# A graph kernel's first stage: the self weights go into the ring from ScalarE in place of POOL

## The chip, the cores and the metric

One core of a Trainium2 chip runs the kernel. The metric is the time of one execution on the device in microseconds (us). The runs of the kernel before took 4477.64, 4478.68 and 4486.39 us: a median of 4478.68.

## The reference

12500 nodes have 256 features each. 212500 edges (two directions of 100000 random pairs, and a self loop for each node) are sorted by their destination. What is computed, cut to what matters:

```python
# first stage (L0)
agg = segment_sum(x[src], dst, N)                     # 212500 rows of 256, float32
z = (1 + eps) * x + agg
z = relu(z @ W1 + b1) @ W2 + b2
z = (z - mean(z, 0)) * rsqrt(var(z, 0) + 1e-5) * gamma + beta + x
x1 = layernorm(x + z)
# second stage (L1)
s = segment_sum(edge_weight[:, None] * x1[src], dst, N)
out = layernorm(x1 + relu(s @ W3))
```

The second stage treats an edge from a node to itself apart: its weight goes on a diagonal. These sums of weights, one for each node, are the "self weights". They are gathered in the first stage, as a 257th column of its matmuls.

## The kernel before, in words

Edges are taken in pairs of chunks, 2 x 128 edges to a pair: 831 pairs, padded to 832. The nodes are 98 tiles of 128. A tile has some 8.5 pairs.

*The ring.* 32 slots of a pair each hold gathered rows of x. POOL fills them with indirect DMAs, two to a pair (gather, L552 to L555), in 26 rounds of 32 pairs. The first round stands ahead of the loop. In the loop (L574 to L587) POOL waits at each half ring for the indices (s_idx), and at each fourth slot for PE to have read the old rows (s_entered). Behind every eighth pair it runs selves_of (L565, L566): a copy of 128 x 16 numbers from self_next into the column ring_self of eight slots. The first four of these copies come from selfT, behind the first 64 gathers.

*SyncE.* follow (L450 to L468) waits for the four groups of eight pairs of a round (s_gathered), then for POOL's copy (s_selfed, L458), and then adds 8 to s_landed (L459), on which PE waits. Behind every second group it loads the next indices and the next self weights (self_next), 16 KB each.

*DVE.* It computes a table with ten numbers for each tile (NEW to SWEEP), which say where the tile's pairs begin and end; entry (L378) loads a tile's numbers into registers of an engine (L380). selfT, the self weights of all pairs, is computed before the first tile (L931 to L936). Then DVE works in blocks of two tiles (block, L1020): the first half of a sort (members), the one-hot matrices of the odd tile (ones_of_tile, L893 on; the operation stands in L901), the second half of the sort (places), and the one-hot matrices of the next even tile. Each set of one-hots has a short operation of 128 x 256 for the pair that two tiles share, one of 128 x 2048 for eight pairs, and a short one. Between the parts of a block stand operations for the sort's earlier block (keyed, L877 on) and the statistics of z (z_stats).

*PE.* sum_tile (L1270) multiplies the one-hots of a tile with the ring's rows and the 257th column (L1284, L1294), waits for s_onehot and s_landed, and puts other small matmuls in between; own adds the tile's own x.

*ACT.* two_tiles (L1675) copies sums out (summed), turns, applies ReLU and bias (hidden_out L1615, z_out L1625), hands the sort's ranks to DVE (ranks_out), and issues DMAs for x, z and the sort's runs. 49 blocks of two tiles make the stage.

After the stage come the normalisation, and the second stage with a like ring and gathers (L619), but without copies on POOL; its table has six numbers for an entry (entry2, L387).

Of the kernel before, what the change touches and what calls it, by code (L numbers as in the profile page):

```python
# [54 lines left out]
def gnn(nc, x, src, dst, edge_weight, w1, b1, w2, b2, gamma, beta, eps_gin, w3, lists, stage_dram, z_dram, x1_dram, out):  # L55
# [29 lines left out]
    with ctx:  # L85
# [48 lines left out]
        self_next = sb("self_next", [P, RING, 2], f32)  # L134
# [46 lines left out]
        row = work[0:1, 4000:4000 + 12 * (NT + 1)].rearrange("p (a t) -> p a t", a=12)  # L181
        row_i = work[0:1, 5200:5200 + 3 * NT].bitcast(i32).rearrange("p (a t) -> p a t", a=3)
        flag = sb("flag", [1, 3], f32)
        table = sb("table", [1, NT, 10], mybir.dt.uint16)
# [220 lines left out]
        NEW, HEAD, M4, M2, END, LOW, REP, SHARED, OFF, SWEEP = range(10)  # L405
# [6 lines left out]
        def _(sp):  # L412
# [37 lines left out]
            def follow(n_sweeps):  # L450

                with sp.Fori(0, n_sweeps) as sweep:
                    with sp.Fori(0, ROUNDS) as i:
                        r = sweep * ROUNDS + i
                        for g in range(4):
                            sp.wait_ge(s_gathered[g], r * (32 * QUARTER) + 32 * QUARTER)
                            stand(sp)
                            sp.wait_ge(s_selfed, r * 4 + g + 1)  # L458
                            sp.sem_inc(s_landed, QUARTER)  # L459
                            if g % 2 == 1:  # L460
                                h = g // 2
                                sp.dma_start(idx[:, h * HALF:(h + 1) * HALF, :],
                                             srcT[:, ds((i + 1) * RING + h * HALF, HALF), :]).then_inc(s_idx[h], 16)
                                sp.dma_start(self_next[:, h * HALF:(h + 1) * HALF, :],
                                             selfT[:, ds((i + 1) * RING + h * HALF, HALF), :]).then_inc(s_idx[h], 16)
                for h in range(2):
                    sp.wait_ge(s_idx[h], n_sweeps * (32 * ROUNDS) + 16)
                stand(sp)  # L468
# [70 lines left out]
        def _(pool):  # L539
# [25 lines left out]
            def selves_of(q, of):  # L565
                nc.gpsimd.tensor_copy(ring_self[:, q:q + QUARTER, :], of[:, q:q + QUARTER, :]).then_inc(s_selfed, 1)  # L566

            pool.wait_ge(s_selves, 1)
            for q in range(0, RING, QUARTER):
                selves_of(q, selfT)  # L570
# [3 lines left out]
            with pool.Fori(1, n_sweeps * ROUNDS) as r:  # L574
                for h in range(2):
                    pool.wait_ge(s_idx[h], r * 32 + 16)
                    stand(pool)
                    for q in range(h * HALF, (h + 1) * HALF):
                        if q % FOUR == 0:

                            pool.wait_ge(s_entered, r * RING + (q - RING + FOUR + 1))
                            stand(pool)
                        for c in range(2):
                            gather(q, c)
                        if (q + 1) % QUARTER == 0:
                            selves_of(q + 1 - QUARTER, self_next)
# [52 lines left out]
        def _(dve):  # L639
# [91 lines left out]
            sync()  # L731
            for column, of in ((NEW, newly), (HEAD, end), (M4, send), (M2, begins), (END, new), (LOW, slo)):
                setup(nc.vector.tensor_tensor(table[0:1, :, column], of, tmp, ALU.subtract))
# [159 lines left out]
            def ones_of_tile(j, bank):  # L893

                new, head, m4, m2, _, _, _, shared, off, sweep = entry(dve, j)
# [27 lines left out]
            def z_stats(m):  # L923
                dve.wait_ge(s_z, m + 1)
                stand(dve)
                for f in range(KH):
# [6 lines left out]
            setup(nc.vector.scalar_tensor_tensor(out=selfT[:, :, :], in0=selfT[:, :, :], scalar=0.0, in1=wT[:, :, :],  # L933
                                                 op0=ALU.is_equal, op1=ALU.mult))
            sync()
            nc.vector.tensor_copy(selfT[:, PADP:PADP + RING, :], selfT[:, 0:RING, :]).then_inc(s_selves, 1)  # L936
# [295 lines left out]
        def _(pe):  # L1232
# [37 lines left out]
            def sum_tile(j, bank, others):  # L1270

                new, head, m4, m2, end, low, rep, _, off, sweep = entry(pe, j)
# [23 lines left out]
                with pe.If(new < m4):  # L1296
                    with pe.Fori(new, m4, 2 * TWO) as p:
                        for b in range(0, 2 * TWO, TWO):
                            pe.wait_ge(s_landed, p + first + (b + TWO))
                            pe.wait_ge(s_onehot, p + counted + (b + TWO + 1))  # L1300
                            add(p + b, loop_of[:, b:b + TWO], TWO).then_inc(s_added, TWO)
                with pe.If(m4 < head):
                    pe.wait_ge(s_landed, m4 + first + TWO)
                    pe.wait_ge(s_onehot, m4 + counted + (TWO + 1))
                    add(m4, loop_of[:, 0:TWO], TWO).then_inc(s_added, TWO)
                pe.wait_ge(s_onehot, head + counted + TILE_ONES)
                pe.wait_ge(s_landed, low + first)
# [119 lines left out]
            pe.sem_inc(s_quarter, PARTS)  # L1427
            for k in range(5):
# [142 lines left out]
        def _(act):  # L1571
# [102 lines left out]

            def two_tiles(k, old, sorts=True, loads=True):  # L1675
# [6 lines left out]
                if loads:  # L1682
                    load_x(k + 1)
# [8 lines left out]
                if old >= 3:  # L1692
                    keep_z(k - 3)

            act.wait_ge(s_table, 1)
            act.wait_ge(s_selves, 1)
            for k in range(5):
# [184 lines left out]
```

## Time and profile before

| what | us |
|---|---|
| median of three runs | 4478.68 |
| the profiled execution, by the device's time | 4476.26 |
| its span in the trace | 4473.0 |
| POOL busy | 3318.0 (74%) |
| PE busy | 3437.8 (77%) |
| DVE busy | 2623.7 (59%) |
| ACT busy | 414.0 (9%) |

The span is that from the first to the last instruction of the trace, and the device's own time is 3.3 us longer. Times in rows are us from the span's start, unless they are marked ns or stand as a mean of one instruction, which is in ns. The first stage runs to about 2262 us, the second begins at 2429 us. An operation marked "DMA_INDIRECT" on POOL is the writing of descriptors for a gather, not the transfer. "issue" is time in which an engine waited for nothing that the profile shows. PEq, DVEq and so on are the sequencers of the engines.

### The profile page before, as it was taken

The numbers are of one execution on the slowest core, as the hardware profiler recorded it, in microseconds if no ns is written. First come the engines' busy times: TensorE is split into PE (matmuls) and PEld (weight loads), VectorE is DVE, ScalarE is ACT, GpSimd is POOL, SyncE is SP. The second block draws the span as 40 slices with busy tenths as digits, with TensorE's granted clock in tenths as the row PEclk, the third lists the DMA queues.
The fourth block names the chain that finished last, engine by engine and source line by source line (L and its number), as shares of the span: only waits on it lengthen the run. The fifth ranks groups of instructions, "written<-read, shape, count | busy, mean of one in ns | idle before, by whom it ended". The sixth has DMA issues, their size and how long they took to land.

```text
span 4473.0 us, 69589 instructions
## 1 busy us (share of the span) xinstructions
PE 3437.8 (77%) x16131; PEld 2829.6 (63%) x16132; DVE 2623.7 (59%) x5747; ACT 414.0 (9%) x1055; POOL 3318.0 (74%) x3456
## 2 busy tenths in 40 slices
PE   2787877877777777787654888888888888888887
PEld 2676766666666666666543666666666666666665
DVE  3888877776787777687656334344434444443443
ACT  0000000000000000000044000000000000000001
POOL 6777777777777777777734777777777777777775
PEclk7888988988988898888866999999999999999999
DMA  5343333433343333333386334434443444334343
GB/s 144 107 114 111 112 112 110 116 112 109 113 115 113 110 112 114 111 111 112 106 266 202 113 113 120 119 115 118 120 119 115 119 120 119 115 119 119 115 119 101
DMA packets 305380, 540.19 MB, mean 121 GB/s; under 512 B 85290, under 2 KB 197790, under 8 KB 305326
## 3 DMA queue, kind: packets, MB, share of 16 engines
q0 software_dynamic: 159424, 434.52, 33.5%
q10 hardware_dynamic: 89348, 67.77, 5.0%
q1 hardware_dynamic: 56554, 37.24, 2.8%
q8 instruction: 26, 0.43, 0.0%
q14 instruction: 28, 0.23, 0.0%
HBM read 489.80 MB, written 46.88 MB: 120 GB/s over the span
## 4 chain that ended last, share of the span: by engine, by line
POOL 62%; issue 22%; PE 5%; DVE 5%; DMA 3%; POOLq 1%; DVEq 1%; ACT 1%; ACTq 0%; SPq 0%; PEldq 0%
POOL ring L619 31%; POOL ring L553 30%; PE ps L1284 2%; PE ps L1494 1%; DMA x_dram<-ring 1%; DMA ring<-x_dram,idx 1%; DVE work L889 1%; POOLq L630 1%; PE ps L1367 1%; DVEq L380 1%; DMA z_dram<-z_pair 1%; DVE work L886 0%; ACT ring L1725 0%; DMA ring<-in_x,idx 0%; POOL ring L566 0%
## 5 line engine op out<-in xcount | busy, mean ns | idle before, releaser
L553 POOL DMA_INDIRECT ring<-in_x,idx x1664 | 1708.6, 1027 | 502.8 <-issue 473.1
L619 POOL DMA_INDIRECT ring<-x_dram,idx x1612 | 1524.0, 945 | 517.7 <-issue 489.8
L1494 PE MATMUL ps<-ring,work 128*128 x6448 | 1521.4, 391 | 339.8 <-SPq L529 337.8
L1494 PEld LDWEIGHTS ps<-ring,work 128*128 128x128 f32 x6448 | 1217.6, 193 | 629.4 <-issue 472.1
L1155 DVE TENSOR_SCALAR work<-ps,dstT,wT 128x256 f32<-128x256 f32 x1612 | 742.2, 539 | 1129.9 <-PE ps L1494 1057.9
L1284 PE MATMUL ps<-ring,ones_sb 128*128 x3324 | 935.8, 431 | 390.2 <-SPq L459 348.5
L1284 PEld LDWEIGHTS ps<-ring,ones_sb 128*128 128x128 f32 x3324 | 694.7, 216 | 549.2 <-issue 443.4
L901 DVE SCALAR_TENSOR_TENSOR ones_sb<-dstT,tile_base,minus_iota 128x256 f32<-128x256 f32 (+1 forms) x294 | 318.5, 1110 | 226.5 <-issue 187.3
L1367 PEld LDWEIGHTS ps<-work 128*128 128x128 f32 x3384 | 429.8, 197 | 17.9 <-DVE work L889 2.9
L1367 PE MATMUL ps<-work 128*128 128x128 f32 x3384 | 428.3, 279 | 2.1 <-DVE work L889 2.1
L886 DVE TENSOR_TENSOR work<-ps,current 128x768 f32<-128x768 f32 x282 | 267.8, 950 | 9.1 <-PE ps L1367 9.1
L889 DVE TENSOR_TENSOR work<-slot_is,ps 128x768 f32<-128x768 f32 x282 | 266.8, 946 | 0.0
L1294 PE MATMUL ps<-ring,ones_sb 128*128 x384 | 116.6, 429 | 61.6 <-issue 34.1
L1786 ACT ACTIVATE work<-ps 128x512 f32<-128x512 f32 x49 | 29.3, 597 | 1448.1 <-PE ps L1524 1448.1
L883 DVE TENSOR_TENSOR slot_is<-ps,current 128x384 f32<-128x384 f32 x282 | 156.0, 553 | 6.7
L1625 ACT ACTIVATE z_pair<-ps,cols 128x256 f32 (+1 forms) x98 | 41.1, 471 | 914.3 <-DVE zstats L927 848.3
L1294 PEld LDWEIGHTS ps<-ring,ones_sb 128*128 128x128 f32 x384 | 68.8, 199 | 86.7 <-issue 80.3
L811 DVE TENSOR_TENSOR ps<-ps,work 128x588 f32<-128x588 f32 x141 | 109.8, 778 | 20.7
L815 DVE TENSOR_REDUCE place_f<-ps 128x12 f32<-128x588 f32 x141 | 108.7, 771 | 20.6
L591 POOL DMA_INDIRECT lists<-work,target x47 | 45.4, 967 | 97.7 <-DMA lists<-work,target 73.1
L1451 PE MATMUL ps<-ident,ones_sb 128*128 128x128 f32 x196 | 47.0, 420 | 85.7 <-DVE ones_sb L1078 69.6
L1347 PE MATMUL ps<-hidT,w2s 128*128 128x256 f32 x392 | 106.3, 397 | 3.6 <-ACT hidT L1615 3.6
(245 smaller groups left out, 2178.6 us busy)
## 6 DMA issues: line engine op xcount, KB each, us to landing
ring<-in_x,idx POOLq DMA_INDIRECT x1664
ring<-x_dram,idx POOLq DMA_INDIRECT x1612, 2.7
z_dram<-z_pair ACTq DMA_DIRECT2D x49, 256.0 KB, 3.2
ones_sb<-x_dram ACTq DMA_DIRECT2D x49, 256.0 KB
ring<-z_dram SPq DMA_DIRECT2D x24, 512.0 KB, 6.0
ring<-in_x SPq DMA_DIRECT2D x24, 512.0 KB, 7.3
x_dram<-ring ACTq DMA_DIRECT2D x24, 512.0 KB, 3.8
out<-ones_sb ACTq DMA_DIRECT2D x48, 256.0 KB
```

Of the source, the lines that this page charges most:

```text
L553: nc.gpsimd.indirect_dma_start(out=ring[:, q, c, :], out_offset=None, in_=x, in_offset=bass.IndirectOffsetOnAxis(ap=idx[:, q, c:c + 1], ax ...
L619: nc.gpsimd.indirect_dma_start(out=ring[:, q, c, :], out_offset=None, in_=x1_dram, in_offset=bass.IndirectOffsetOnAxis(ap=idx[:, q, c:c + ...
L811: nc.vector.tensor_tensor(p_sel, p_base[:, q:q + 1, 0:NBK].to_broadcast([P, SPAN, NBK]), member[:, q * SPAN:(q + 1) * SPAN, :], ALU.mult). ...
L883: nc.vector.tensor_tensor(slot_is[:, q % 2, :, :], p_iota[:, 0:SLOTS].unsqueeze(1).to_broadcast([P, WIDTH, SLOTS]), current[:, 1, mine].un ...
L886: nc.vector.tensor_tensor(of_run[:, q, :, :], p_iota.unsqueeze(1).to_broadcast([P, WIDTH, P]), current[:, 0, mine].unsqueeze(2).to_broadca ...
L889: nc.vector.tensor_tensor(values[:, q, :, :, :], slot_is[:, q % 2, :, :].unsqueeze(3).to_broadcast([P, WIDTH, SLOTS, 2]), p_packed[:, :, m ...
L901: return nc.vector.scalar_tensor_tensor(out=to.rearrange("p b c n -> p (b c) n"), in0=dstT[:, ds(at, n), :].rearrange("p b c -> p (b c)"). ...
L1155: last = nc.vector.tensor_scalar(to[:, b, c, :], bucket_nodes, dstT[:, ds(at + b, 1), c], wT[:, ds(at + b, 1), c], ALU.is_equal, ALU.mult)
L1284: last = nc.tensor.matmul(wide, ones_of[:, b, c, :], summands[:, ds((p + b) & (RING - 1), 1), c, :].rearrange("p a d -> p (a d)"), start=F ...
L1294: nc.tensor.matmul(wide, shared_of[bank][:, 0, c, :], summands[:, ds((new + (RING - 1)) & (RING - 1), 1), c, :].rearrange("p a d -> p (a d)"),
L1367: last = nc.tensor.matmul(p_pack, of_run[:, q, c, :], values[:, q, c, :, :].rearrange("p n f -> p (n f)"), start=(q == 0 and c == 0), stop ...
L1494: last = nc.tensor.matmul(to[:, t * D:(t + 1) * D], ones_of[:, b, c, t * P:(t + 1) * P], ring[:, ds((p + b) & (RING - 1), 1), c, :].rearra ...
```

## The change

POOL makes no copies any more, and self_next, its 52 loads and SyncE's wait for the copies are gone. selfT is no longer continued beyond its end (the copy in L936 goes). The table has two more numbers for each tile, FROM and UPTO: the first and the last block of eight pairs that begins in the tile. ACT has a function selves, which loads the tile's entry, and for each such block waits until PE has read the slots' old rows, and copies 128 x 16 numbers from selfT into the ring. It is called for tiles 0 and 1 ahead of the loop, for tile 2k + 2 behind summed(k, 0), and for tile 2k + 3 at the end of two_tiles(k). PE waits for s_selfed itself. PE adds 32 to s_entered at its start, and the terms of POOL's wait change to match. All of PE's, DVE's and ACT's entry loads bring twelve numbers.

```diff
-        NEW, HEAD, M4, M2, END, LOW, REP, SHARED, OFF, SWEEP = range(10)
+        NEW, HEAD, M4, M2, END, LOW, REP, SHARED, OFF, SWEEP, FROM, UPTO = range(12)
...
                             sp.wait_ge(s_gathered[g], r * (32 * QUARTER) + 32 * QUARTER)
-                            stand(sp)
-                            sp.wait_ge(s_selfed, r * 4 + g + 1)
                             sp.sem_inc(s_landed, QUARTER)
...
-                                sp.dma_start(self_next[:, h * HALF:(h + 1) * HALF, :],
-                                             selfT[:, ds((i + 1) * RING + h * HALF, HALF), :]).then_inc(s_idx[h], 16)
...
-            def selves_of(q, of):
-                nc.gpsimd.tensor_copy(ring_self[:, q:q + QUARTER, :], of[:, q:q + QUARTER, :]).then_inc(s_selfed, 1)
-
-            pool.wait_ge(s_selves, 1)
-            for q in range(0, RING, QUARTER):
-                selves_of(q, selfT)
...
-                            pool.wait_ge(s_entered, r * RING + (q - RING + FOUR + 1))
+                            pool.wait_ge(s_entered, r * RING + (q + FOUR + 1))
                             stand(pool)
                         for c in range(2):
                             gather(q, c)
-                        if (q + 1) % QUARTER == 0:
-                            selves_of(q + 1 - QUARTER, self_next)
...
+            setup(nc.vector.scalar_tensor_tensor(out=from_i, in0=newly, scalar=float(QUARTER - 1), in1=tmp, op0=ALU.add, op1=ALU.subtract))
+            setup(nc.vector.scalar_tensor_tensor(out=upto_i, in0=new, scalar=float(QUARTER - 1), in1=tmp, op0=ALU.add, op1=ALU.subtract))
+            sync()
+            setup(nc.vector.tensor_scalar(from_i, from_i, 3, None, ALU.arith_shift_right))
+            setup(nc.vector.tensor_scalar(upto_i, upto_i, 3, None, ALU.arith_shift_right))
+            sync()
+            setup(nc.vector.tensor_copy(table[0:1, :, FROM], from_i))
+            setup(nc.vector.tensor_copy(table[0:1, :, UPTO], upto_i))
...
+                            stand(pe)
+                            pe.wait_ge(s_selfed, ((p + (b + TWO + QUARTER - 1)) >> 3) + sweep * 4)
                             add(p + b, loop_of[:, b:b + TWO], TWO).then_inc(s_added, TWO)
...
                 pe.wait_ge(s_onehot, head + counted + TILE_ONES)
+                stand(pe)
+                pe.wait_ge(s_selfed, upto + sweep * 4)
+                stand(pe)
                 pe.wait_ge(s_landed, low + first)
...
             pe.sem_inc(s_quarter, PARTS)
+            pe.sem_inc(s_entered, RING)
...
+            def selves(j):
+
+                *_, sweep, begin, upto = entry(act, j)
+                with act.If(begin < upto):
+                    with act.Fori(begin, upto) as b:
+                        act.wait_ge(s_entered, b * QUARTER + sweep * RING + (QUARTER + 1))
+                        stand(act)
+                        nc.scalar.activation(ring_self[:, ds((b & 3) * QUARTER, QUARTER), :], selfT[:, ds(nc.s_assert_within(b, 0, ROWS // QUARTER - 1, skip_runtime_bounds_check_because=IN_RANGE) * QUARTER, QUARTER), :], ACT.Copy).then_inc(s_selfed, 1)
+
             def two_tiles(k, old, sorts=True, loads=True):
...
                 summed(k, 0)
                 if loads:
+                    selves(2 * k + 2)
                     load_x(k + 1)
...
                     keep_z(k - 3)
+                if loads:
+                    selves(2 * k + 3)
 
             act.wait_ge(s_table, 1)
             act.wait_ge(s_selves, 1)
+            selves(0)
+            selves(1)
```

## Rows read from the trace of the kernel before

**Rows 1.** The page, part 4: the chain that ended last, shares by engine.

```profile
POOL 62%; issue 22%; PE 5%; DVE 5%; DMA 3%; POOLq 1%; DVEq 1%; ACT 1%; ACTq 0%; SPq 0%; PEldq 0%
```

**Rows 2.** Window of the first stage; columns: PE, PEld, DVE, ACT, POOL, PEclk, DMA.

```profile
90.00:2262.00 2172.00, 1674.13 (x8513) 1409.24 (x8514) 1634.04 (x3295) 166.22 (x524) 1669.13 (x1709) 0.87 0.39 112
```

**Rows 3.** Groups on POOL, 105 to 2235 us: busy, mean ns, idle before.

```profile
L553 POOL DMA_INDIRECT ring<-in_x,idx x1595 | 1636.7, 1026 | 470.7 <-issue 452.7 <-PE ps L1284 4.0
L566 POOL COPY ring<-self_next 128x16 f32<-128x16 f32 x99 | 23.2, 234 | 0.3
```

**Rows 4.** Waits, 105 to 2235 us: total us, times, longest us.

```profile
PE ps L1284 <- SPq L459: 301.3, 62, 14.3
...
POOL ring L553 <- PE ps L1284: 4.0, 13, 0.3
```

**Rows 5.** Second stage, the gathers: min/median/max ns, first and last start.

```profile
L619 POOL DMA_INDIRECT ring<-x_dram,idx x1612: 942/946/963, 2429.3 to 4443.1; - x180
```

**Rows 6.** Timeline of POOL, start us and us, around one copy.

```profile
1019.28 0.95 POOL L553 DMA_INDIRECT ring<-in_x,idx  x1 [0.30 <-issue]
1020.24 0.22 POOL L566 COPY ring<-self_next 128x16 f32<-128x16 f32 x1
...
1021.89 0.94 POOL L553 DMA_INDIRECT ring<-in_x,idx  x1 [0.31 <-issue]
```

**Rows 7.** Timeline of POOL, then of PE, at the start of the first stage.

```profile
93.30 0.61 POOL L566 COPY ring<-selfT 128x16 f32<-128x16 f32 x4
101.68 0.97 POOL L553 DMA_INDIRECT ring<-in_x,idx  x1 [7.77 <-PE ps L1284]
...
94.19 9.68 PE L1284 MATMUL ps<-ring,ones_sb 128*128 x36 [47.26 <-SPq L459]
```

**Rows 8.** Waits of SyncE's queue: us, times, longest.

```profile
SPq L459 <- POOL ring L566: 49.7, 1, 49.7
```

**Rows 9.** DVE by form, 105 to 2235 us: the long one-hot.

```profile
L901 DVE SCALAR_TENSOR_TENSOR ones_sb<-dstT,tile_base,minus_iota 128x2048 f32<-128x2048 f32 x96 | 227.2, 2366 | 4.3
```

**Rows 10.** Timeline of DVE: sets of one-hots, three early, two late.

```profile
408.77 3.32 DVE L901 SCALAR_TENSOR_TENSOR ones_sb<-dstT,tile_base,minus_iota 128x256 f32<-128x256 f32 x3 [2.81 <-issue]
...
426.59 3.29 DVE L901 SCALAR_TENSOR_TENSOR ones_sb<-dstT,tile_base,minus_iota 128x256 f32<-128x256 f32 x3 [1.02 <-issue]
...
451.42 3.33 DVE L901 SCALAR_TENSOR_TENSOR ones_sb<-dstT,tile_base,minus_iota 128x256 f32<-128x256 f32 x3 [2.82 <-issue]
...
2117.29 3.32 DVE L901 SCALAR_TENSOR_TENSOR ones_sb<-dstT,tile_base,minus_iota 128x256 f32<-128x256 f32 x3 [2.81 <-issue]
...
2135.10 3.29 DVE L901 SCALAR_TENSOR_TENSOR ones_sb<-dstT,tile_base,minus_iota 128x256 f32<-128x256 f32 x3 [1.01 <-issue]
```

**Rows 11.** Timeline of POOL beside the first two of these sets.

```profile
410.63 1.89 POOL L553 DMA_INDIRECT ring<-in_x,idx  x1 [0.30 <-issue]
...
426.70 1.19 POOL L553 DMA_INDIRECT ring<-in_x,idx  x1 [0.30 <-issue]
428.20 2.10 POOL L553 DMA_INDIRECT ring<-in_x,idx  x1 [0.30 <-issue]
```

**Rows 12.** One more set, DVE, and the gather beside it, POOL.

```profile
641.72 3.29 DVE L901 SCALAR_TENSOR_TENSOR ones_sb<-dstT,tile_base,minus_iota 128x256 f32<-128x256 f32 x3 [1.65 <-issue]
...
642.55 2.87 POOL L553 DMA_INDIRECT ring<-in_x,idx  x1 [0.30 <-issue]
```

**Rows 13.** Loads of a table entry, DVE: L380 ten values, L387 six.

```profile
L380 DVEq TENSOR_LOAD <-table x98: 2264/2270/3010, 48.2 to 2194.4; - x98
...
L387 DVEq TENSOR_LOAD <-table x49: 1383/1389/1398, 2425.5 to 4399.7; - x49
```

**Rows 14.** Timeline of ACT: two operations and the waits that end at them.

```profile
625.85 0.84 ACT L1615 ACTIVATE hidT<-ps,cols 128x256 f32<-128x256 f32 x2 [15.01 <-PE ps L1334]
...
652.59 0.84 ACT L1625 ACTIVATE z_pair<-ps,cols 128x256 f32 x2 [16.02 <-DVE zstats L927]
```

**Rows 15.** Chain in order of time near the end of the first stage.

```profile
2193.95 3.64 DMA ring<-in_x,idx
```

More of the change, by code:

```diff
@@ L133, in gnn @@
         minus_iota = sb("minus_iota", [P, P], f32)
-        self_next = sb("self_next", [P, RING, 2], f32)
         ranks_f = sb("ranks_f", [P, THIRDS + 1, NB1], f32)
@@ L180, in gnn @@
         unsorted_p = sb("unsorted_p", [P, 1], f32)
-        row = work[0:1, 4000:4000 + 12 * (NT + 1)].rearrange("p (a t) -> p a t", a=12)
-        row_i = work[0:1, 5200:5200 + 3 * NT].bitcast(i32).rearrange("p (a t) -> p a t", a=3)
+        row = work[0:1, 4000:4000 + 14 * (NT + 1)].rearrange("p (a t) -> p a t", a=14)
+        row_i = work[0:1, 5400:5400 + 5 * NT].bitcast(i32).rearrange("p (a t) -> p a t", a=5)
         flag = sb("flag", [1, 3], f32)
-        table = sb("table", [1, NT, 10], mybir.dt.uint16)
+        table = sb("table", [1, NT, 12], mybir.dt.uint16)
         sweeps = sb("sweeps", [1, 1], i32)
@@ L463, in follow @@
                                              srcT[:, ds((i + 1) * RING + h * HALF, HALF), :]).then_inc(s_idx[h], 16)
-                                sp.dma_start(self_next[:, h * HALF:(h + 1) * HALF, :],
-                                             selfT[:, ds((i + 1) * RING + h * HALF, HALF), :]).then_inc(s_idx[h], 16)
                 for h in range(2):
-                    sp.wait_ge(s_idx[h], n_sweeps * (32 * ROUNDS) + 16)
+                    sp.wait_ge(s_idx[h], n_sweeps * (16 * ROUNDS) + 16)
                 stand(sp)
@@ L575, in _ @@
                 for h in range(2):
-                    pool.wait_ge(s_idx[h], r * 32 + 16)
+                    pool.wait_ge(s_idx[h], r * 16 + 16)
                     stand(pool)
@@ L731, in _ @@
             sync()
+            from_i, upto_i = row_i[:, 3, :], row_i[:, 4, :]
+            setup(nc.vector.scalar_tensor_tensor(out=from_i, in0=newly, scalar=float(QUARTER - 1), in1=tmp, op0=ALU.add, op1=ALU.subtract))
[6 more added lines that the diff above has]
+            setup(nc.vector.tensor_copy(table[0:1, :, UPTO], upto_i))
             for column, of in ((NEW, newly), (HEAD, end), (M4, send), (M2, begins), (END, new), (LOW, slo)):
@@ L893, in ones_of_tile @@
             def ones_of_tile(j, bank):
-                new, head, m4, m2, _, _, _, shared, off, sweep = entry(dve, j)
+                new, head, m4, m2, _, _, _, shared, off, sweep, _, _ = entry(dve, j)
                 counted = sweep * RING + off
@@ L932, in _ @@
             sync()
[L933 to L936, printed above, removed]
+            nc.vector.scalar_tensor_tensor(out=selfT[:, :, :], in0=selfT[:, :, :], scalar=0.0, in1=wT[:, :, :],
+                                           op0=ALU.is_equal, op1=ALU.mult).then_inc(s_selves, 1)
             dve.wait_ge(s_selves, 1)
@@ L1270, in sum_tile @@
             def sum_tile(j, bank, others):
-                new, head, m4, m2, end, low, rep, _, off, sweep = entry(pe, j)
+                new, head, m4, m2, end, low, rep, _, off, sweep, _, upto = entry(pe, j)
                 first = sweep * RING
@@ L1304, in sum_tile @@
                     pe.wait_ge(s_onehot, m4 + counted + (TWO + 1))
+                    stand(pe)
+                    pe.wait_ge(s_selfed, ((m4 + (TWO + QUARTER - 1)) >> 3) + sweep * 4)
                     add(m4, loop_of[:, 0:TWO], TWO).then_inc(s_added, TWO)
                 pe.wait_ge(s_onehot, head + counted + TILE_ONES)
+                stand(pe)
+                pe.wait_ge(s_selfed, upto + sweep * 4)
+                stand(pe)
                 pe.wait_ge(s_landed, low + first)
```

## The prediction

> **What bounds the kernel now.** Read first the chain of waits: POOL holds 62% of it and "issue", the steps between POOL's instructions, most of the next 22% [rows 1]. Then the window of the first stage, 90 to 2262 us: POOL and PE are both about 77% busy, DVE 75%, ACT 8% [rows 2], so shares don't tell the bound. The waits do: PE waits 301 us for SyncE's report that rows have landed, POOL waits for PE 4.0 us in 13 places, each no longer than its usual gap [rows 4]. POOL sets the pace, by the number of gathers it can start.
>
> A gather's price is clearest in the second stage, where nothing else runs on POOL: (4443.1 - 2429.3) / 1611 = 1.25 us from start to start [rows 5]. In the first stage 1595 gathers take 2130 us, 1.335 us each. Two things explain the difference: the copies and the pauses. The pauses are 1636.7 us of busy time less 1595 x 0.946 [rows 3, 5] = 128 us; take off some 3 us for the slightly longer gather after each copy, and 125 us are left. They fall beside DVE's long one-hot operation, 96 times in the window, 2.37 us each [rows 9]: 1.30 us per tile. Each tile has one set of three L901 operations: a short one, the long one, a short one.
>
> **The parts of the change.**
>
> *Start of the stage.* POOL's four first copies stand at 93.30, behind its first 64 gathers; SyncE waits 49.7 us for them before it reports any landing [rows 8], PE begins at 94.19, and POOL then waits 7.77 us for PE to free slots [rows 7]. ACT can copy as soon as DVE's weights are ready, right before DVE's first entry load at 48.2 us [rows 13]; ACT's own load and the set of one-hots that PE needs too (load 2.3 to 2.7 us, set 3.3 us) end near 56, so PE begins there and is through tile 0 long before POOL needs the slots. POOL goes on at 93.6 in place of 101.68: -8.1 us. DVE's new operations on the 98-entry table (six, plus waits, some 1.5 us) and ACT's first two entries lie under POOL's first 64 gathers, and would cost PE's start no more than that if they did not.
>
> *100 copies inside the loop.* With a copy between, two gathers take 1021.89 - 1019.28 = 2.61 us instead of 2.50 [rows 6]: 0.11 us, not its 0.22 us of duration, as half of it fills the usual gap. 100 x 0.11 = -11 us. What POOL still waits for in these places (s_idx, s_entered) costs nothing: the second stage has the same kind of waits and a pitch of 1.25 throughout.
>
> *SyncE's queue.* 52 small loads and their waits go, and the wait for the copies; the landing reports come no later. Nothing else stands in that queue, and PE's waits are for gathers: 0.
>
> *ACT.* Two entry loads per block of two tiles, and 104 copies of 128 x 16. The nearest prices are DVE's load (2.27 us for ten values, [rows 13]) and POOL's copy (0.23 us, [rows 3]): some 3.5 us per tile. Behind them in ACT's queue are L1615 and L1625, which wait 15.0 and 16.0 us for PE and for DVE [rows 14]; these waits cover it. Without that cover see the third rival.
>
> *PE.* It gains waits on s_selfed, a longer entry load and register work, below 1 us per tile, under its 301 us of waits for landings. Only in the last tiles, where the chain runs through it from a landing at 2193.95 + 3.64 [rows 15], do I add 0.5 us. All of that tail follows the last gathers and so moves with POOL.
>
> *DVE and its effect on POOL.* This is the term that decides. Each tile's entry grows from ten values to twelve. The load takes 2.270 us for ten and 1.389 us for six [rows 13], 0.22 us a value, so 2.71 us for twelve: 0.44 us more before each set of one-hots. DVE alone can take it: its block of two tiles lasts (451.42 + 3.33) - (408.77 + 3.32) = 42.66 us when it waits for nothing, POOL's share of a block (831 pairs / 49 blocks x 2 x 1.335) is 45.3 us. But the pauses depend on where the long one-hot falls in POOL's 1.25 us cycle. POOL always resumes 0.73 us after a set's end: 412.09 and 412.82, 429.88 and 430.60, 645.01 and 645.72 [rows 10 to 12]. It then keeps its cycle until the next set. So the loss at a set is 0.72 us plus the remainder of (interval between set ends - 0.73 - 0.10 per copy) by 1.25; a remainder under about 0.2 counts with a whole 1.25 on top, for I find losses from 0.94 to 2.1. The rule gives 1.43 for the interval of 17.79 us and 1.01 for 24.87; the rows show 0.25 + 1.15 = 1.40 and 0.94, and 1.93 for a set that comes at another phase [rows 11, 12]. Of 95 intervals 32 are 17.8 us and 25 are 24.8 to 25.0, from the sets at 408.77 and 426.59 to those at 2117.29 and 2135.10 [rows 10].
>
> After the change they are 18.23 and 25.31 with no copy inside. (18.23 - 0.73) = 14 x 1.25 + 0.00: a loss of 1.97. (25.31 - 0.73) = 19 x 1.25 + 0.83: a loss of 1.55. So 32 x (1.97 - 1.40) + 25 x (1.55 - 0.94) = 33.5 us are lost again; I take 30, since DVE, no longer behind at the start, will have some six fewer regular intervals. The other 38 stay at their present mean. If the load cost nothing more, the missing copies alone would give 1.53 and 1.11: +8 us; with every phase equally likely the mean loss is 1.55 against 1.30: +24 us. All these are losses, because the present phases are among the best. Bounds of this term: 0 and +45.
>
> **Sum**, against the profiled execution's own 4476.3 us (span 4473.0): -8.1 - 11 + 30 + 0.5 = +11.4, that is 4487.7 us. The median of the runs shown, 4478.68, is 2.4 us higher; between the two I put the forecast at 4489 us.
>
> **Rivals.**
> 1. *The pauses keep their mean.* For it: the number of sets does not change. Against it: the arithmetic above, which fits the rows to 0.1 us. Time: 4476.3 - 19.1 + 2.4 = 4460 us, faster. The Trainium skill, "SBUF — State Buffer", section "Who interferes with whom", has a VectorE instruction with two SBUF inputs and a GpSimd instruction that reads SBUF exclude each other, the first to issue holding the ports for its whole length. The trace agrees that L901 stops gathers; a reader who only counts such instructions gets 98 before and after and would forecast this rival.
> 2. *The phases scatter*, because ACT's new loads coincide with DVE's and stretch them; DVE's take up to 3.01 us already [rows 13]. Then -19.1 + 24 + 0.5: 4482 to 4484 us, no difference that can be told.
> 3. *ACT becomes part of DVE's loop.* Place: the entry load of selves(2k + 3), between DVE's z statistics and ranks_f. It decides once ACT's 16.0 us of cover are gone. Price: DVE's block becomes 42.66 + 0.88 + 3.5 = 47.0 us against 45.3, times 47: about 4560 us. [rows 14] speak against it.
> 4. *PE does not begin earlier*, as something else holds tile 0. Then 8.1 us of gain are missing from any case.
>
> **How the numbers follow.** About 0.2% (9 us) is what a measurement of this kernel can tell from no change. The forecast has 0.48 and its own range 4480 to 4500 us; scattered phases 0.22; kept pauses 0.21; ACT in the loop 0.04; a late PE 0.05. Faster by over 0.2% (below 4469.7): nearly all of rival 1, 0.21. Slower by over 0.2% (above 4487.6): some two thirds of the forecast, a quarter of rival 2, rival 3, 0.43. Within: 0.36. The range that holds 8 in 10 takes in rival 1 at its lower end: 4459 to 4501 us.
>
> **What would show it.** In the profile after: PE's first L1284 near 56 us; POOL's first gather of the second round at about 93.6, no copy on POOL; 1.25 us between gathers outside the pauses; DVE's L380 load at 2.71 us; set intervals of 18.2 and 25.3 us; and a mean L553 gather above 1.026 us, near 1.04 to 1.05, where rival 1 has 1.02. The forecast is wrong if that mean does not rise, if the load's price does not grow with the values, or if PE's waits for landings disappear.

## The result and the profile after

The changed kernel takes 4496.85 us (median of 8 runs, 4493.98 to 4503.77), the kernel before in the same series 4483.6 us (8 runs, 4477.64 to 4488.28): a ratio of 1.0032, interval 1.0021 to 1.0043. It is 13.3 us slower. The profiled execution took 4497.28 us against 4476.26, a difference of 21.0 us, since the profiled execution of before was faster than all eight of its runs, 7.3 us below their median. What follows accounts for the difference of the two profiles; in the medians it is 13.3.

The page's chain and the window of the first stage, which answer to [rows 1, 2]:

```profile
POOL 64%; issue 22%; PE 7%; DMA 3%; POOLq 1%; ACT 1%; DVE 1%; ACTq 0%; SPq 0%; DVEq 0%; PEldq 0%
```

```profile
90.00:2262.00 2172.00, 1662.37 (x8330) 1398.38 (x8329) 1612.42 (x3256) 182.61 (x601) 1680.72 (x1606) 0.86 0.38 110
```

POOL is still what the chain hangs on. In the same 2172 us it is busy longer (1680.72 against 1669.13), though its copies are gone and it issued fewer gathers (1578 against 1595 from 105 to 2235 us). The group of gathers, 105 to 2235 us, as in [rows 3], then all gathers of the two stages (min/median/max ns, first and last start):

```profile
L548 POOL DMA_INDIRECT ring<-in_x,idx x1578 | 1652.6, 1047 | 480.6 <-issue 475.2 <-PE ps L1278 5.5
```

```profile
L548 POOL DMA_INDIRECT ring<-in_x,idx x1664: 942/946/3065, 7.0 to 2258.7; - x185
...
L606 POOL DMA_INDIRECT ring<-x_dram,idx x1612: 942/946/962, 2452.1 to 4465.9; - x180
```

A gather of the first stage now takes 1047 ns on average in place of 1026, at the same median of 946. The last one starts at 2258.7 us; before it was 2237.5. The second stage takes (4465.9 - 2452.1) = 2013.8 us, the same as in [rows 5] to 0.1 us. The waits of the stretch, which answer to [rows 4]:

```profile
POOL ring L548 <- issue: 475.2, 1560, 0.3
...
PE ps L1278 <- SPq L456: 271.6, 60, 14.5
...
PE ps L1278 <- DVE ones_sb L897: 10.0, 2, 7.9
...
PE ps L1278 <- ACT ring L1684: 10.8, 3, 5.7
```

PE still waits mostly for landings, and for ACT's copies (L1684) only 10.8 us in three places. The start of the stage, POOL, then DVE's third set of one-hots, then PE, then ACT; before, POOL ran its four copies at 93.30 and then waited until 101.68 [rows 7]:

```profile
84.30 2.91 POOL L548 DMA_INDIRECT ring<-in_x,idx  x1 [0.30 <-issue]
...
91.28 0.95 POOL L548 DMA_INDIRECT ring<-in_x,idx  x1 [0.30 <-issue]
92.53 0.95 POOL L548 DMA_INDIRECT ring<-in_x,idx  x1 [0.30 <-issue]
93.78 0.95 POOL L548 DMA_INDIRECT ring<-in_x,idx  x1 [0.30 <-issue]
95.03 0.95 POOL L548 DMA_INDIRECT ring<-in_x,idx  x1 [0.30 <-issue]
...
97.53 0.95 POOL L548 DMA_INDIRECT ring<-in_x,idx  x1 [0.30 <-issue]
```

```profile
83.50 3.29 DVE L897 SCALAR_TENSOR_TENSOR ones_sb<-dstT,tile_base,minus_iota 128x256 f32<-128x256 f32 x3 [3.09 <-issue]
```

```profile
58.19 2.08 PE L1278 MATMUL ps<-ring,ones_sb 128*128 x4 [8.15 <-ACT ring L1684]
```

```profile
53.70 0.23 ACT L1684 ACTIVATE ring<-selfT  x1 [23.79 <-issue]
54.45 0.23 ACT L1684 ACTIVATE ring<-selfT  x1 [0.53 <-issue]
57.83 0.23 ACT L1684 ACTIVATE ring<-selfT  x1 [3.14 <-issue]
```

The 7.77 us of waiting are gone. The gather at 97.53 is POOL's 65th, the first of the second round, which began at 101.68 before. It comes only 4.1 us earlier because DVE's third set, at 117.71 before, now falls among the first 64 gathers: the gather at 84.30 takes 2.91 us. The number of sets is 98 as before. The loads of a table entry on the three engines, to [rows 13], in ns:

```profile
L379 PEldq TENSOR_LOAD <-table x98: 2850/2856/3045, 46.6 to 2272.1; - x98
L379 ACTq TENSOR_LOAD <-table x98: 2535/2582/3457, 50.2 to 2267.9; - x98
L379 DVEq TENSOR_LOAD <-table x98: 2703/2710/3494, 50.5 to 2213.7; - x98
```

Three sets of one-hots on DVE in a row, and the gathers of POOL beside them:

```profile
1157.78 3.29 DVE L897 SCALAR_TENSOR_TENSOR ones_sb<-dstT,tile_base,minus_iota 128x256 f32<-128x256 f32 x3 [1.46 <-issue]
...
1183.14 3.27 DVE L897 SCALAR_TENSOR_TENSOR ones_sb<-dstT,tile_base,minus_iota 128x256 f32<-128x256 f32 x3 [3.25 <-issue]
...
1201.35 3.29 DVE L897 SCALAR_TENSOR_TENSOR ones_sb<-dstT,tile_base,minus_iota 128x256 f32<-128x256 f32 x3 [1.46 <-issue]
```

```profile
1158.61 2.89 POOL L548 DMA_INDIRECT ring<-in_x,idx  x1 [0.30 <-PE ps L1278]
1161.81 0.95 POOL L548 DMA_INDIRECT ring<-in_x,idx  x1 [0.30 <-issue]
...
1184.41 2.43 POOL L548 DMA_INDIRECT ring<-in_x,idx  x1 [0.30 <-issue]
1187.14 0.94 POOL L548 DMA_INDIRECT ring<-in_x,idx  x1 [0.30 <-issue]
...
1202.16 2.90 POOL L548 DMA_INDIRECT ring<-in_x,idx  x1 [0.30 <-issue]
1205.36 0.95 POOL L548 DMA_INDIRECT ring<-in_x,idx  x1 [0.30 <-issue]
```

The sets end at 1161.07, 1186.41 and 1204.64: intervals of 25.3 and 18.2 us. POOL goes on 0.74, 0.73 and 0.72 us after each end. The gather caught takes 2.89, 2.43 and 2.90 us instead of 0.95, losses of 1.94, 1.48 and 1.95 us. In [rows 11] the same two kinds of set cost 0.94 and 1.40.

**Where the 22.5 us of span went.** For every two neighbouring gathers of a trace I took the time from start to start less 1.25 us, and put it to a set of one-hots where one lies beside them:

| us | before | after | difference |
|---|---|---|---|
| beside the 98 sets | 125.9 | 163.7 | +37.8 |
| copies on POOL, and its wait at the start | 18.1 | 0 | -18.1 |
| other, start of the first gather | | | +1.5 |
| last gather to the end of the first stage | 24.4 | 27.5 | +3.1 |
| between the stages | 167.4 | 165.9 | -1.5 |

The sum is +22.8, against 22.5 in the spans (the rest is rounding). Of the 18.1 us the start is 8.1 and the 100 copies 10.0. The mean loss of a set rose from 1.28 to 1.67 us (96 and 95 sets). The difference by the device's time is 21.0 us and not 22.5, because that time is 3.3 us longer than the span before and 1.8 us after.

One thing is needed to read the experiments. They were measured in six series, each with the kernel before beside it, and each kernel is compared only with the kernel before of its own series. In five of the six the clock granted to TensorE was lower, 0.82 of full speed on average in place of 0.90, and the kernel before took 5376 to 5398 us in place of 4482. One of these five and the one at 0.90 report the same chip number, so it need not belong to a chip. The two levels are called "the low clock" and "the full clock" below; where an expectation speaks of two kinds of chip, it is these two. They are names and not a cause: among the eight runs of the changed kernel in the first series one had a mean granted clock of 0.797 and took 4503.77 us, only 7 us above the median. The changed kernel itself was never measured at the low clock.

### The profile page after: what moved, and what is told of

Same layout as the page of the kernel before. It is cut to its first block, busy times and chain, and to the rows that moved or that the text cites. A ratio compares the mean times of both kernels' runs of the same rounds, so it can differ in the third digit from the quotient of the medians.

```text
span 4495.5 us, 70641 instructions
## 1 busy us (share of the span) xinstructions
PE 3471.4 (77%) x16131; PEld 2855.9 (64%) x16132; DVE 2613.0 (58%) x5752; ACT 438.8 (10%) x1160; POOL 3331.5 (74%) x3352
## 4 chain that ended last, share of the span: by engine, by line
POOL 64%; issue 22%; PE 7%; DMA 3%; POOLq 1%; ACT 1%; DVE 1%; ACTq 0%; SPq 0%; DVEq 0%; PEldq 0%
POOL ring L548 32%; POOL ring L606 32%; PE ps L1278 4%; DMA ring<-in_x,idx 1%; PE ps L1368 1%; DMA x_dram<-ring 1%; PE ps L1496 1%; POOLq L617 1%; DMA z_dram<-z_pair 0%; DMA ring<-x_dram,idx 0%; ACT ring L1741 0%; PE ps L1348 0%; PE ps L1335 0%; POOLq L618 0%; PE ps L1288 0%
## 5 line engine op out<-in xcount | busy, mean ns | idle before, releaser
L548 POOL DMA_INDIRECT ring<-in_x,idx x1664 | 1746.0, 1049 | 510.5 <-issue 501.0
L1278 PE MATMUL ps<-ring,ones_sb 128*128 x3324 | 958.2, 439 | 359.1 <-SPq L456 280.8
L1278 PEld LDWEIGHTS ps<-ring,ones_sb 128*128 128x128 f32 x3324 | 711.1, 222 | 523.3 <-issue 412.4
L1368 PEld LDWEIGHTS ps<-work 128*128 128x128 f32 x3384 | 429.6, 197 | 14.8
L1368 PE MATMUL ps<-work 128*128 128x128 f32 x3384 | 427.6, 279 | 0.0
L1288 PE MATMUL ps<-ring,ones_sb 128*128 x384 | 117.0, 431 | 38.0 <-issue 36.4
L1273 PE MATMUL ps<-zeros 1*128 1x257 bf16 x98 | 26.3, 268 | 147.4 <-issue 113.6
L1348 PE MATMUL ps<-hidT,w2s 128*128 128x256 f32 x392 | 117.3, 430 | 3.0 <-ACT hidT L1617 3.0
```

Of the source, the lines that this page charges most:

```text
L548: nc.gpsimd.indirect_dma_start(out=ring[:, q, c, :], out_offset=None, in_=x, in_offset=bass.IndirectOffsetOnAxis(ap=idx[:, q, c:c + 1], ax ...
L1278: last = nc.tensor.matmul(wide, ones_of[:, b, c, :], summands[:, ds((p + b) & (RING - 1), 1), c, :].rearrange("p a d -> p (a d)"), start=F ...
L1288: nc.tensor.matmul(wide, shared_of[bank][:, 0, c, :], summands[:, ds((new + (RING - 1)) & (RING - 1), 1), c, :].rearrange("p a d -> p (a d)"),
L1348: last = nc.tensor.matmul(p_out[:, f * 2 * P:(f + 1) * 2 * P], w2s[:, k, f * P:(f + 1) * P], hidT[:, k, :], start=(k == 0), stop=(k == KH ...
L1368: last = nc.tensor.matmul(p_pack, of_run[:, q, c, :], values[:, q, c, :, :].rearrange("p n f -> p (n f)"), start=(q == 0 and c == 0), stop ...
```

## The experiments

**1. VectorE loads ten values again, all else as changed.** This takes back the one part that the forecast blames.

```diff
-        def entry(eng, j):
+        def entry(eng, j, first=0, upto=12):
...
-                table[0:1, ds(j, 1), :]
+                table[0:1, ds(j, 1), first:upto]
...
-                new, head, m4, m2, _, _, _, shared, off, sweep, _, _ = entry(dve, j)
+                new, head, m4, m2, _, _, _, shared, off, sweep = entry(dve, j, 0, 10)
```

> The changed kernel, but DVE loads only the first ten numbers of a tile's entry; PE and ACT still load twelve. Phase theory: the two regular intervals between sets of one-hots go back to about 17.8 and 24.9 us, without copies between them, so the losses per set become 0.72 + 0.81 = 1.53 and 0.72 + 0.39 = 1.11 us in place of 1.95 and 1.34 to 1.48; the mean over all sets falls from 1.67 to about 1.35 us, 98 sets bring back some 30 us: about 4467 us, below the kernel before. Rival (the time comes from ACT's loads, from PE's longer path or from the end of the stage, DVE's load being covered by its slack): no change against 4497 us.

At the low clock: 5434.57 us against 5389.89, a ratio of 1.0104 (1.0016 to 1.0191). Neither theory is judged by it, because POOL is not what it waits for there:

```profile
L548 POOL DMA_INDIRECT ring<-in_x,idx x1315 | 1342.7, 1021 | 803.6 <-issue 378.5 <-PE ps L1278 261.1 <-remote 164.0
```

```profile
PE 43%; issue 25%; another core or an unknown queue 16%; DVE 8%; DVEq 4%; DMA 1%; ACT 1%; ACTq 1%; POOL 0%; SPq 0%; POOLq 0%; PEldq 0%
```

POOL waits 261 us for PE, and 164 us for something that the profile does not name ("remote", in the chain "another core or an unknown queue"), where it waited 4.0 us before [rows 4]; its share of the chain is 0% against 62% [rows 1]. So the same kernel ran again in another series:

> The same kernel as e1_dve_loads_ten, since in that call every kernel, the one before too, ran at 5340 us and more with waits that no engine of the core explains. Where the kernel before runs near 4484 us, the expectations are as they were. Phase theory: intervals 17.8 and 24.9 us, losses 1.53 and 1.11 us, mean loss per set 1.35 in place of 1.67 us, about 4467 us. Rival: the time of the changed kernel, 4497 us.

At the full clock: **4466.83 us** (6 runs, 4464.35 to 4472.64) against 4481.78 (9 runs), a ratio of 0.9968, interval 0.9955 to 0.998. Its profile, POOL's group as above, the load, and one set with a gather beside it (the set's three operations in one row of a source line, ns; the gathers in the timeline):

```profile
L548 POOL DMA_INDIRECT ring<-in_x,idx x1594 | 1640.3, 1029 | 485.6 <-issue 481.3 <-PE ps L1278 4.3
```

```profile
L379 DVEq TENSOR_LOAD <-table x98: 2264/2271/3032, 50.4 to 2183.1; - x98
```

```profile
L897 DVE SCALAR_TENSOR_TENSOR ones_sb<-dstT,tile_base,minus_iota x3: 480/488/2350, 459.6 to 462.4; 128x256 f32<-128x256 f32 x2, 128x2048 f32<-128x2048 f32 x1
```

```profile
460.83 2.43 POOL L548 DMA_INDIRECT ring<-in_x,idx  x1 [0.30 <-issue]
463.56 0.95 POOL L548 DMA_INDIRECT ring<-in_x,idx  x1 [0.30 <-issue]
```

The intervals are back at 17.8 (34 times, mean loss 1.51 us), 24.9 (12 times, 1.04) and 24.8 us (8 times, 0.95); the prediction gave 1.53 and, for 24.87, 1.11 for exactly this case, the missing copies without the longer load. The time beside the 98 sets is 134.6 us against 163.7 with twelve values: 29.1 us less. The ratios, 1.0032 and 0.9968, differ by 0.64%, that is 28.7 us; they come from two series, and each is good to some 0.12%, 5 us. So the two extra values in VectorE's load cost some 29 us, and everything else in the change gains 15 us. At the full clock this version is faster than both kernels.

**2. The load alone, on the kernel before.** Two columns of zeros more in the table, and VectorE alone loads twelve.

```diff
-        table = sb("table", [1, NT, 10], mybir.dt.uint16)
+        table = sb("table", [1, NT, 12], mybir.dt.uint16)
...
-                new, head, m4, m2, _, _, _, shared, off, sweep = entry(dve, j)
+                new, head, m4, m2, _, _, _, shared, off, sweep, _, _ = entry(dve, j, 0, 12)
```

> The kernel before, with two unused numbers added to the table, which DVE alone loads (twelve in place of ten); copies stay on POOL, PE loads ten. Phase theory: intervals 18.23 and 25.31 us with a copy in each, remainders 1.15 and 0.73, losses 1.87 and 1.45 us in place of 1.42 and 0.95; 32 x 0.45 + 25 x 0.50 = 27 us more: about 4511 us. Rival (0.88 us per block is covered by DVE's slack of 2.6 us per block): 4484 us, no change.

> The same kernel as e2_before_loads_twelve, on a chip that may run as in the traces: the kernel before, DVE alone loading twelve numbers. Phase theory: intervals 18.2 and 25.3 us with a copy in each, losses 1.87 and 1.45 us in place of 1.42 and 0.95: 27 us more, about 4509 us. Rival (DVE's slack covers it): 4482 us.

> The kernel before (its copies still on GpSimd) with two unused values more in VectorE's load per round, 12 in place of 10, timed again because the two earlier times fell on a chip where TensorE's pace hid all of it. Theory (each set costs a load of 2.71 us in place of 2.27 us, so the sets stand 18.2 and 25.3 us apart as in the changed kernel and the gathers lose about 1.67 us a set in place of 1.28 us): with its 100 copies left as they are, 98 sets by about 0.4 us is 38 us, so about 4515 us and a ratio near 1.008, sets at 18.2 and 25.3 us, 120 to 165 us of excess in long gathers. Rival (the two values cost nothing by themselves, and the longer pauses of the changed kernel come from ScalarE's copies and loads): 4480 to 4488 us, a ratio of 1.000 to 1.002, with sets at 17.8 and 24.9 us or with losses that stay at 1.28 us a set.

All three fell on the low clock: ratios of 0.9996 (0.996 to 1.0033), 1.0004 (0.9967 to 1.0041) and 0.9996 (0.9953 to 1.0039). They do not decide, for the reason seen above; the load of the third, and POOL's group, 105 to 2235 us:

```profile
L380 DVEq TENSOR_LOAD <-table x98: 698/2708/3497, 80.2 to 2649.3; - x98
```

```profile
L553 POOL DMA_INDIRECT ring<-in_x,idx x1347 | 1380.0, 1024 | 728.6 <-issue 382.3 <-PE ps L1285 196.9 <-remote 144.1
```

What they do show: the load alone takes 2.71 us and moves the commonest interval of two sets to 18.2 us (21 of 80, 14 of 78 and 23 of 78 sets in the three profiles) without ScalarE having any part in it; and 0.44 us more per tile on VectorE costs nothing that can be told, to some 20 us, where POOL has 340 us of waits to spare. The time of the load alone at the full clock stays unmeasured.

**3. The loop's copies alone.** The kernel before without the copies in the loop, their loads and SyncE's wait for them; the self weights of all pairs but the first 32 are left out. SyncE waits once, ahead of its first report, for the four copies that stay.

```diff
-                            sp.wait_ge(s_selfed, r * 4 + g + 1)
...
-                                sp.dma_start(self_next[:, h * HALF:(h + 1) * HALF, :],
-                                             selfT[:, ds((i + 1) * RING + h * HALF, HALF), :]).then_inc(s_idx[h], 16)
...
-                        if (q + 1) % QUARTER == 0:
-                            selves_of(q + 1 - QUARTER, self_next)
```

> The kernel before without the 100 copies inside POOL's loop and without their loads and waits on SyncE; the first four copies stay, and so does the late start. It leaves out the self weights of all but the first 32 pairs. Counting only: 100 x 0.10 = -10 us: 4474 us. Phase theory: -10 us, but the regular losses go from 1.42 and 0.95 to 1.53 and 1.11 us, 32 x 0.11 + 25 x 0.16 = +8 us: about 4481 us, and the mean loss per set rises from 1.28 to about 1.37 us.

At the low clock: 5397.09 us, a ratio of 1.0024 (0.999 to 1.0059). No gain and no loss that can be told; POOL waits 223.2 us for PE in it. Whether 10 us come free at the full clock was not measured alone; the first experiment holds it only together with the start of the stage.

**4. One value more.** The changed kernel with a table of 14 columns, of which VectorE loads 13.

```diff
-        table = sb("table", [1, NT, 12], mybir.dt.uint16)
+        table = sb("table", [1, NT, 14], mybir.dt.uint16)
...
-                new, head, m4, m2, _, _, _, shared, off, sweep, _, _ = entry(dve, j)
+                new, head, m4, m2, _, _, _, shared, off, sweep, _, _, _ = entry(dve, j, 0, 13)
```

> The changed kernel with a 13th, unused number in the table, loaded by DVE only: its load grows from 2.71 to 2.93 us, DVE's block by 0.44 us. Phase theory: intervals 18.44 and 25.5 us, remainders 0.21 and about 1.0; the first stands at the point where the loss jumps from 2.1 down to 0.94, the second gives 1.75. If it lands below the jump, the sum of a pair of losses falls from 3.4 to 2.7 us, some 20 us less: about 4477 us, although every step of DVE is longer; if above, the losses are about 2.15 and 1.75 and the time is about 4510 us. Rival (a longer load costs by its length, or nothing): 4497 to 4510 us with the mean loss unchanged at 1.67 us.

> The same kernel as e7_dve_loads_thirteen: the changed kernel, DVE alone loading 13 numbers. Phase theory: intervals 18.44 and 25.5 us, the first at the point where the loss jumps from 2.1 down to 0.94 us, the second with 1.6 to 1.75. Below the jump: about 4477 us; above: about 4510 us. Rival (a longer load costs nothing or its length): 4497 to 4510 us with the mean loss unchanged at 1.67 us.

At the low clock, twice: 1.0064 (1.0028 to 1.01) and 1.0056 (1.0019 to 1.0094). Beside the 1.0104 of ten values there, the number that VectorE loads makes no difference that can be told at this clock, while what ten and thirteen have in common, the rest of the change, costs 0.6 to 1.0%. A candidate is PE: its own load grew from 2.389 us to 2.856, which is 0.47 us for each of 98 tiles or 46 us, 0.85% of 5390 us, and experiment 2, in which PE still loads ten, shows no loss. That is a fit, not a test: PE's load was not changed alone. At the full clock, thirteen values were not measured either.

**5. Where the pauses come from.** The one-hots' second operand is read from PSUM (where the same row of numbers already stands), with the sign of dstT changed, there and in the four other places that write or read it, so that the values fit. Of the edit the operation itself:

```diff
-                        scalar=base, in1=minus_iota[:, :].unsqueeze(1).to_broadcast([P, 2 * n, P]), op0=ALU.add, op1=ALU.is_equal)
+                        scalar=base, in1=p_iota.unsqueeze(1).to_broadcast([P, 2 * n, P]), op0=ALU.subtract, op1=ALU.is_equal)
```

> The changed kernel, with the one-hots' second input (the row of node numbers) read from PSUM, where the sort keeps it already, in place of SBUF; to that end dstT holds the destinations with a plus sign, and the four places that read it have their signs changed. L901's form then has one input in SBUF. If the pauses come from two SBUF inputs: gathers run beside the one-hots at 1.25 us, mean loss below 0.2 us, the first stage is bound by DVE's block (43.5 us x 47) or by POOL's 42.4 us: the last gather 120 us or more earlier at best, 70 to 110 us once DVE sets the pace: 4390 to 4425 us. Rival (any long DVE operation, or its writing, holds up the gathers; or the pauses are DVE waiting for POOL): mean loss stays above 1.2 us, 4490 to 4505 us.

> The same kernel as e5_one_hot_from_psum, on a chip that may run as in the traces. There no gather was longer beside a set of one-hots (0 of 98, before 98 of 98), but PE set the pace and the time was 3% above the kernel before. Phase theory, where POOL sets the pace: 163 us of pauses gone, then DVE's block of 43.5 us or POOL's 42.4 us bounds the stage, 4390 to 4425 us. Rival, from the other chip: taking the pauses away makes something else late (PE waits for PSUM or for DVE), and the time is 4500 us or more.

And the same with a table in another order, of which VectorE loads seven values and ScalarE three:

```diff
-        NEW, HEAD, M4, M2, END, LOW, REP, SHARED, OFF, SWEEP, FROM, UPTO = range(12)
+        NEW, HEAD, M4, M2, SHARED, OFF, SWEEP, FROM, UPTO, END, LOW, REP = range(12)
...
-                new, head, m4, m2, _, _, _, shared, off, sweep, _, _ = entry(dve, j)
+                new, head, m4, m2, shared, off, sweep = entry(dve, j, 0, 7)
...
-                *_, sweep, begin, upto = entry(act, j)
+                sweep, begin, upto = entry(act, j, 6, 9)
```

> As e5_one_hot_from_psum, and the table is put in another order so that DVE loads only the seven numbers it reads and ACT three; PE loads twelve. With the pauses gone the phase says nothing any more, and DVE's block falls from 43.5 to 42.66 - 2 x 3 x 0.22 = 41.3 us, under POOL's 42.4 us: POOL is the bound, 831 pairs x 2.50 us. About 20 to 40 us less than e5, 4375 to 4395 us. If the pauses stay (the rival of e5): intervals of 17.1 and 24.2 us, near the jump, anything from 4470 to 4510 us.

> The changed kernel with the one-hots' second operand read from PSUM and a load of 7 values in place of 12, once more. On a chip at which the kernel before takes about 4480 us, GpSimd sets the pace; there the theory that the pauses are the price of the one-hots' second SBUF operand expects the 163.7 us of the sets' pauses to go, less what TensorE's matmuls and the results' turns then hold back (271.6 us of waits for landings in the changed kernel show that TensorE has some slack, not how much): 4350 to 4430 us, ratio 0.97 to 0.99. Rival: TensorE's clock falls with the denser stream of matmuls and takes all of it back: 4480 to 4620 us, with GpSimd waiting for TensorE by over 100 us in the chain of waits. On a chip at which the kernel before takes about 5385 us: 1.026 again, no gather lengthened beside a set.

At the low clock all four are slower: 1.0313 (1.0249 to 1.0378) and 1.0298 (1.025 to 1.0347) with the PSUM operand, 1.0262 (1.0194 to 1.0329) and 1.0247 (1.0167 to 1.0327) with the short loads too. But the mechanism is plain in the profiles. POOL's group of the last of the four, the load, and the one-hots (min/median/max ns):

```profile
L548 POOL DMA_INDIRECT ring<-in_x,idx x1264 | 1200.4, 950 | 946.0 <-PE ps L1278 442.2 <-issue 368.1 <-remote 135.7
```

```profile
L379 DVEq TENSOR_LOAD <-table x98: 537/1608/2243, 96.6 to 2804.1; - x98
...
L897 DVE SCALAR_TENSOR_TENSOR ones_sb<-dstT,tile_base,ps x225: 473/481/2349, 110.2 to 2223.6; 128x256 f32<-128x256 f32 x76, 128x2048 f32<-128x2048 f32 x37
```

The mean gather is 950 ns, against 1024 in the kernel of experiment 2 at the same clock: not one gather beside a set is lengthened in any of the four profiles of this experiment, where the third of experiment 2 has 91 such gathers with 116.8 us of excess in them. The long one-hot itself takes 2.35 us as before. So the pauses belong to the second SBUF operand of L901 and to nothing else that runs at that time. The Trainium skill, "SBUF — State Buffer", section "Who interferes with whom", names as the condition two SBUF inputs on VectorE and a GpSimd instruction that reads SBUF. The gather reads its row numbers (idx) from SBUF, and the runs agree. The same section infers that a two-input operation such as tensor_tensor leaves the generation of descriptors alone, as that needs the write side. The measurement decides against that for this pair, scalar_tensor_tensor and an indirect gather: with two SBUF operands the writing of descriptors is lengthened beside all 98 sets of the changed kernel, by up to 1.95 us in the rows above.

The time did not follow. POOL's waits for PE doubled (442.2 us against 196.9), and PE's own waits do not name a cause. PE in the second profile of the first form, 1012 to 1024 us:

```profile
1012.65 0.38 PE L1278 MATMUL ps<-ring,ones_sb 128*128 x1 [0.98 <-issue]
1014.78 0.38 PE L1278 MATMUL ps<-ring,ones_sb 128*128 x1 [1.75 <-issue]
1016.90 0.59 PE L1278 MATMUL ps<-ring,ones_sb 128*128 x1 [1.74 <-issue]
1019.71 0.59 PE L1278 MATMUL ps<-ring,ones_sb 128*128 x1 [2.22 <-issue]
1022.50 0.58 PE L1261 MATMUL ps<-x_pair,self_term 128*128 x1 [2.21 <-issue]
```

Matmuls stand alone, some 2.1 to 2.8 us apart, in which PE waits for nothing that the profile shows. Such gaps before L1278 are 53 in 2130 us with 44.7 us in the changed kernel at the full clock, and 167 with 217.0 us in this profile:

```profile
PE ps L1278 <- issue: 217.0, 167, 7.0
PE ps L1368 <- issue: 183.0, 145, 3.1
```

Experiment 2 has them too (349.6 us in 283 places before its L1285, 95.4 before its L1368). Over all of PE's operations, from 105 us to the stage's last gather, they sum to 121 us in the kernel before and 178 in the changed one at the full clock; at the low clock to 701 in the third of experiment 2, 750 in experiment 1, and 850 to 875 in the four profiles with the PSUM operand. Their last gather comes at 2800 to 2838 us, against 2646 and 2697. So the time lost is about what these gaps grew by. Some records may be missing from the trace, so a gap can hide a matmul, but not the longer time. What makes the gaps, and why they grow when POOL is freed, is open, and so is what these versions would give at the full clock: all four of their series fell on the low one.

## Why the prediction was right

The forecast was 4489 us, slower by 10.3 on the median of the runs shown (11.4 on the profiled execution), with a range of 4459 to 4501; 4496.85 came out, on a before of 4483.6: slower by 13.3. The mechanism is the one that the prediction named, but that the numbers lie so close is in part luck: between the two profiles on which it was worked out the difference is 21.0 us (22.5 in the spans), twice the forecast. By its steps:

- *Start of the stage.* Forecast -8.1 us; the wait of 7.77 us and the four copies are gone. But the sign that was named, POOL's first gather of the second round at about 93.6, did not come: it begins at 97.53. Of the 3.9 us, 1.97 are the third set of one-hots, which now falls ahead of it, 0.7 are the larger losses at the first two sets (1.39 and 1.64 against 1.18 and 1.20), and the rest lies ahead of them; the table counts them with the sets and under "other". PE begins at 58.19, not near 56: the set of one-hots ends at 56.91 and the trace names ACT's third copy, 57.83 + 0.23, as what released it. It costs nothing.
- *Copies in the loop.* Forecast -11, measured -10.0 by the ledger.
- *SyncE, PE, ACT.* Forecast 0. PE's waits for landings are still 271.6 us; ACT's copies ended a wait of PE three times. This holds at the full clock. At the low clock, where PE sets the pace, the rest of the change costs 0.6 to 1.0%: the cover that the prediction named, those waits of PE for landings, is what is gone there.
- *The load.* Forecast 2.71 us for twelve values, measured 2.710 (the median of 98).
- *The pauses.* Forecast +30 within 0 to +45, measured +37.8. Intervals and losses of the regular sets are as computed: 18.2 us with 1.95 (forecast 1.97), 25.3 us with 1.48 (forecast 1.55), 25.2 with 1.33. The part that was mis-sized is the other sets: the prediction kept them at their present mean, and it rose from 1.36 (42 sets) to 1.61 us (46), some 11 us. 1.61 is near the 1.55 that the prediction itself worked out for phases that are equally likely; why these sets had stood better than that before was not taken apart.
- *The rule for a loss.* The prediction computes a set's loss from its interval. The three profiles at the full clock allow a test on 97 intervals each, regular or not (with a computed loss under 0.93 us raised by 1.25). It comes within 0.1 us of the measured loss for 84 sets before, 90 after and 91 in experiment 1; the computed means are 1.32, 1.70 and 1.39 us, the measured ones 1.29, 1.67 and 1.38. So it is the phase that sets the price of a collision: the length of the load matters by where it puts the next set.
- *The tail.* Forecast +0.5, measured +3.1. The prediction let all of the tail follow the last gathers. Before, it did not: the chain left POOL at 2193.95 [rows 15], 43.6 us ahead of its last gather, and went on through PE and DVE. After, it runs through the last gather at 2258.67.
- *The mean gather.* 1047 ns, in the 1.04 to 1.05 that was given; the first rival had 1.02.

The two terms that were too small, 7.8 and 2.6 us, and 1.0 us less from the copies, are what separates the ledger's 22.8 from 11.4; the two terms that nobody forecast, +1.5 and -1.5, cancel. That the medians differ by only 13.3 goes back mostly to the one execution of before, 7.3 us under its median; where in it that lies can't be seen from one profile, so a part of the 37.8 us may belong to it.

The first rival (pauses keep their mean) falls with the mean gather and with experiment 1. The second (phases scatter) is wrong as the main cause: about half of the sets, 49 of 95, stand at 18.2, 25.2 or 25.3 us, with their own losses, and ten values bring back 17.8 and 24.9. For the other half it describes the mean loss well (1.61 against 1.55). The third falls at the full clock by the waits. The fourth by PE's start.

## What to carry to other kernels

Where one engine stops another for a whole instruction, as L901 stops a gather here, the price of a collision depends on its phase, and a kernel whose two engines have settled into a rhythm can lose 0.4 us a collision through a change of 0.4 us that lies on no critical path. Count the values that an engine loads into registers per iteration, and give each engine the slice it reads: here, at the full clock, the same move of work is 0.3% slower with twelve values and 0.3% faster with ten. At the low clock it was slower by 0.6 to 1.0% with ten or thirteen, so the gain holds only where POOL sets the pace. And an engine with two SBUF operands beside a POOL that writes descriptors is worth one look at whether one operand can come from PSUM; but try it at the clock at which the kernel will run.

## What the runs showed of the hardware that was not expected

- One kernel had two levels of time from series to series: 4482 us at a granted clock near 0.90 and 5376 to 5398 us near 0.82, 20% more time for 9% less clock. The mean clock alone does not set the level, as the run of 4503.77 us at 0.797 shows. The second stage stretches as well, from 2013.8 us to 2410.7 (5298.8 - 2888.1 in the third run of experiment 2), at nearly the same median of a gather, 949 ns against 946.
- At the lower level, changes that free POOL made the kernel 2.5 to 3.1% slower, with stretches in which single matmuls stand some 2 us apart.
- The pause of a gather vanishes entirely with one of the two operands in PSUM (0 lengthened gathers beside the sets in four profiles), while the one-hot keeps its 2.35 us.
